# Layer-2 graph sums as three bf16 products, and a message stage with its work moved from VectorE to ScalarE and POOL

## The reference

```python
xn = _layernorm(x, axis=-1)
norm_src = lax.rsqrt(clip(out_deg, 1.0)); norm_dst = lax.rsqrt(clip(in_deg, 1.0))
h_src = xn * norm_src[:, None]
agg = segment_sum(h_src[src], dst)           # sum of messages over a node's in-edges
out = elu((agg * norm_dst[:, None]) @ weight + bias)
```

## Time and profile before

| | |
|---|---|
| Runs of the kernel | 3095.96 us median of 3 (3094.58 to 3096.4) |
| Profiled execution | 3084.4 us, of which the span from first to last instruction is 3082.8 |
| TensorE matmuls (PE) | 2428.9 us busy, 79% of the span |
| Weight loads (PEld) | 1938.2 us, 63% |
| VectorE (DVE) | 1182.7 us, 38% |
| ScalarE (ACT) | 1085.2 us, 35% |
| POOL | 597.3 us, 19% |
| Granted TensorE clock, mean | 0.879 of full speed |

### The profile page before, as it was taken

The page is one execution under the profiler, slowest core; times in us unless marked ns, Lnnn a source line. Parts: engine busy times, 40 slices in busy tenths (PEclk is TensorE's granted clock), DMA queues, the critical chain, the costliest instruction groups (busy, mean ns, idle before and its releaser), DMA issues.

```text
span 3082.8 us, 39405 instructions
## 1 busy us (share of the span) xinstructions
PE 2428.9 (79%) x11905; PEld 1938.2 (63%) x11906; DVE 1182.7 (38%) x2571; ACT 1085.2 (35%) x2028; POOL 597.3 (19%) x482
## 2 busy tenths in 40 slices
PE   0776799989889798876699557968888897925887
PEld 0444688877768677664588435646666666614776
DVE  4444677754635446332001242323342524230111
ACT  3222577755646556532232221121212111112222
POOL 1610011100100101012122111111313223023554
PEclk9887799999898898977799778978989897957999
DMA  3321011110100201024222233212122212053443
GB/s 121 92 79 55 24 45 43 33 63 31 58 31 18 71 30 60 28 80 111 81 75 65 81 129 106 72 47 70 45 70 58 74 46 78 7 142 67 84 86 63
DMA packets 162717, 202.09 MB, mean 66 GB/s; under 512 B 59801, under 2 KB 131120, under 8 KB 162581
## 3 DMA queue, kind: packets, MB, share of 16 engines
q0 software_dynamic: 75168, 89.11, 12.5%
q1 hardware_dynamic: 75834, 100.45, 9.8%
q10 hardware_dynamic: 11578, 10.82, 1.1%
HBM read 108.51 MB, written 93.74 MB: 66 GB/s over the span
## 4 chain that ended last, share of the span: by engine, by line
PE 42%; DMA 38%; another core or an unknown queue 7%; DVE 4%; ACT 3%; issue 2%; SPq 1%; POOL 1%; ACTq 0%; DVEq 0%; POOLq 0%
PE bank L713 39%; DMA agg_rows<-agg_t 34%; PE bank L719 3%; DMA arena<-agg_rows 1%; POOL w_adj L565 1%; SPq L403 1%; DMA xg<-expert_rows 1%; DMA arena<-in_x 1%; DMA feat<-xg 1%; ACT count_a L1167 0%; ACT w_qc L1167 0%; ACT agg_t L1184 0%; DVE arena L1879 0%; ACT w_adj L1166 0%
## 5 line engine op out<-in xcount | busy, mean ns | idle before, releaser
L713 PE MATMUL bank<-xg,w_adj 125*125 125x256 f32 (+1 forms) x2500 | 656.9, 401 | 0.0
L713 PEld LDWEIGHTS bank<-xg,w_adj 125*125 125x125 f32 x2500 | 458.3, 196 | 64.7 <-issue 1.2
L713 PEld LDWEIGHTS bank<-arena,row_hot 128*125 128x125 f32 x3200 | 423.2, 198 | 88.2 <-issue 68.0
L713 PE MATMUL bank<-arena,row_hot 128*125 128x100 f32 x3200 | 431.0, 281 | 47.1 <-remote 19.6
L719 PE MATMUL bank<-ident,arena 125*128 125x125 f32 (+1 forms) x650 | 139.1, 337 | 338.0 <-remote 178.6
L713 PE MATMUL bank<-t,w_h 128*128 128x250 f32 (+1 forms) x1184 | 325.8, 428 | 17.6 <-remote 11.4
L719 PEld LDWEIGHTS bank<-ident,arena 125*128 125x128 f32 (+1 forms) x650 | 85.1, 167 | 389.3 <-issue 383.2
L1560 DVE TENSOR_TENSOR row_hot<-iota_all,arena 128x2000 f32<-128x2000 f32 x100 | 223.7, 2237 | 224.7 <-PE bank L713 221.8
L1166 ACT ACTIVATE w_adj<-bank 125x200 f32<-125x200 f32 x400 | 217.5, 544 | 259.3 <-PE bank L713 254.0
L713 PEld LDWEIGHTS bank<-t,w_h 128*128 128x128 f32 x1184 | 229.6, 199 | 109.9 <-issue 57.9
L713 PE MATMUL bank<-w_adj,arena 128*125 128x256 f32 x1024 | 241.5, 394 | 0.0
(11 more groups left out here) (322 smaller groups left out, 2939.1 us busy)
## 6 DMA issues: line engine op xcount, KB each, us to landing
count_a<-counts POOLq DMA_DIRECT2D x25, 781.2 KB, 6.3
sorted_in<-pad_rows POOLq DMA_DIRECT2D x16, 878.4 KB, 16.9
arena<-sorted_in SPq DMA_DIRECT2D x49, 251.0 KB
counts<-count_a SPq DMA_DIRECT2D x13, 781.2 KB
counts<-w_qc SPq DMA_DIRECT2D x12, 781.2 KB
arena<-rows_b SPq DMA_DIRECT2D x5, 1875.0 KB
w_adj<-in_L_ffn_Wd POOLq DMA_DIRECT2D x8, 1024.0 KB, 6.2
w_adj<-in_L_ffn_W POOLq DMA_DIRECT2D x16, 512.0 KB, 5.8
```

The source lines that it names most:

```text
L713: return pe.matmul(o, w, r, start=first, stop=last, skip_group_check=not check)
```

## The change

Part 1, the sums of layer 1. `adj1` is a bf16 tile, into which the counts are loaded without a cast; the tiles `count_cur[0]` and the semaphores around it are no longer used there. The messages are split into three bf16 parts whose sum is the fp32 number: `part0` = bf16(m), `part1` = bf16(m - part0), `part2` = the rest. `part0` (with the column of ones) and `part1` lie in the space of `xg`, `part2` in the upper half of `w_adj`. Each product becomes three bf16 matmuls into the same bank. The first two count loads are issued together, ahead of the message stage; the load for block b + 1 is issued behind the gather of block b as before, but with no load one block further ahead. Instead of clearing a semaphore, `aggregate` waits for the number of loads landed (`nth`).

Part 2, the message stage. ScalarE takes the root with epsilon as its bias straight from the variances, normalises `h` into `n_big`, makes the fp32 messages in one of two staging tiles (`stage`, in the space of `row_hot`), and copies them as bf16 to `part0`. POOL makes the two other parts (`message_parts`). VectorE keeps the residual sum, the statistics and two small ops. SP stores `feat1` from the staging tile. TensorE's projection steps wait for `msg_full` where they waited for `nodes_full`.

```diff
+        adj1 = [w_adj[0:B, NB * 64 * i:NB * 64 * (i + 1)].bitcast(BF16).rearrange("p (c d) -> p c d", c=NB) for i in range(2)]
+        part2 = w_adj[0:B, NB * 128:NB * 256].bitcast(BF16).rearrange("p (c d) -> p c d", c=NB)
+        parts = xg[:, 0:NB, :].bitcast(BF16)
+        part0, part1 = parts[:, :, 0:D + 1], parts[:, :, D + 2:2 * D + 2]
...
             for s in range(NS):
                 sp.wait_ge(msg_full, s + 1)
-                sp.dma_start(rows(feat1, s), xg[:, G * s:G * s + G, 0:D]).then_inc(msg_stored, 16)
+                sp.dma_start(rows(feat1, s), stage[s % 2]).then_inc(msg_stored[s % 2], 16)
...
             def adjacency_in(b):
 
-                pool.wait_ge(count_in, 16 * (b + 1))
                 if b >= 2:
                     take(pool, adj_used[b % 2])
-                pool.tensor_copy(adj[b % 2], count_cur[0]).then_inc(counts_copied, 1)
-                take(pool, counts_copied)
-                pool.sem_inc(adj_in[b % 2], 1)
-                if b + 1 < NB:
-                    counts_in(b + 1)
+                pool.dma_start(flat(adj1[b % 2]), counts[b * B:b * B + B, :]).then_inc(adj_in[b % 2], 16)
+
+            def message_parts(s):
+
+                at = slice(G * s, G * s + G)
+                pool.wait_ge(msg_full, s + 1)
+                pool.memset(part0[:, at, D:D + 1], 1.0)
+                chain(pool.tensor_tensor(rest, stage[s % 2], part0[:, at, 0:D], ALU.subtract))
+                chain(pool.tensor_copy(part1[:, at, :], rest))
+                chain(pool.tensor_tensor(part2[:, at, :], rest, part1[:, at, :], ALU.subtract))
+                pool.sem_inc(parts_made, 1)
+                chain.restart()
...
             pool.wait_ge(counts_kept, 1)
-            counts_in(0)
-            adjacency_in(0)
-            pool.wait_ge(msg_stored, 16 * NS)
+            for b in range(2):
+                adjacency_in(b)
+            for s in range(NS):
+                message_parts(s)
+            for k in range(2):
+                pool.wait_ge(msg_stored[k], 16 * ((NS + 1 - k) // 2))
...
-                            mm(ps_agg[0:B, 0:cols], adj[par][:, c, 0:B], xg[:, c, 0:cols], False, False, False)
+                            if layer == 0:
+                                mm(ps_agg[0:B, 0:D], adj[par][:, c, 0:B], xg[:, c, 0:D], False, False, False)
+                            else:
+                                mm(ps_agg[0:B, 0:D + 1], adj1[par][:, c, 0:B], part0[:, c, :], False, False, False)
+                                mm(ps_agg[0:B, 0:D], adj1[par][:, c, 0:B], part1[:, c, :], False, False, False)
+                                mm(ps_agg[0:B, 0:D], adj1[par][:, c, 0:B], part2[:, c, :], False, False, False)
...
             def project1(s):
 
-                pe.wait_ge(nodes_full, s + 1)
+                pe.wait_ge(msg_full, s + 1)
...
                 if s == 0:
-                    pe.wait_ge(msg_full, NS)
-                aggregate(s, s % 2, 1, total)
+                    pe.wait_ge(parts_made, NS)
+                aggregate(s, s % 2, 1, total, nth=s // 2)
...
             def messages(s):
 
+                take(act, act_in)
+                act.activation(sd[:, :], mv[:, :, 1], ACT.Sqrt, bias=eps[:, :]).then_inc(act_out, 1)
                 act.wait_ge(nodes_full, s + 1)
                 for i in range(G):
                     b = G * s + i
-                    last = act.activation(xg[:, b, 0:D], n_big[:, b, :], ACT.Copy, scale=inv_out[:, b:b + 1])
+                    last = act.activation(n_big[:, b, :], h_big[:, b, :], ACT.Identity, bias=shift[:, i:i + 1],
+                                          scale=rs[:, i:i + 1])
                 chain(last)
+                if s >= 2:
+                    act.wait_ge(msg_stored[s % 2], 16 * (s // 2))
+                    act.wait_ge(parts_made, s - 1)
+                for i in range(G):
+                    b = G * s + i
+                    last = act.activation(stage[s % 2][:, i, :], n_big[:, b, :], ACT.Copy, scale=inv_out[:, b:b + 1])
+                chain(last)
+                chain(act.activation(part0[:, G * s:G * s + G, 0:D], stage[s % 2], ACT.Copy))
                 act.sem_inc(msg_full, 1)
...
                 chain(last)
-                norm(n, h)
+                norm_sums(h)
+                dve.sem_inc(act_in, 1)
+                take(dve, act_out)
+                chain(dve.reciprocal(rs[:, :], sd[:, :]))
+                chain(stt(out=shift[:, :], in0=mv[:, :, 0], scalar=-1.0, in1=rs[:, :], op0=ALU.mult, op1=ALU.mult))
                 dve.sem_inc(nodes_full, 1)
```

More of the change, by code:

```diff
@@ L186, in program @@
         adj = [w_adj[0:B, NB * 128 * i:NB * 128 * (i + 1)].rearrange("p (c d) -> p c d", c=NB) for i in range(2)]
+        adj1 = [w_adj[0:B, NB * 64 * i:NB * 64 * (i + 1)].bitcast(BF16).rearrange("p (c d) -> p c d", c=NB) for i in range(2)]
+        part2 = w_adj[0:B, NB * 128:NB * 256].bitcast(BF16).rearrange("p (c d) -> p c d", c=NB)
+        parts = xg[:, 0:NB, :].bitcast(BF16)
+        part0, part1 = parts[:, :, 0:D + 1], parts[:, :, D + 2:2 * D + 2]
+        stage_all = row_hot[0:B, :, :, :].rearrange("p k j n -> p (k j n)")
+        stage = [stage_all[:, G * D * k:G * D * k + G * D].rearrange("p (i d) -> p i d", i=G) for k in range(2)]
+        rest = stage_all[:, 2 * G * D:3 * G * D].rearrange("p (i d) -> p i d", i=G)
         near_i = w_adj[0:B, 0:NB * B].bitcast(I32).rearrange("p (b e) -> p b e", e=B)
@@ L258, in program @@
         st2 = sb("st2", [128, 2])
+        eps, shift = sb("eps", [B, 1]), sb("shift", [B, G])
         table_of = sb("table_of", [1, 1])
@@ L549, in _ @@
             chain(pool.tensor_copy(ident_b[:, :], ident[:, :]))
+            chain(pool.memset(eps[:, :], LN_EPS))
             chain(pool.memset(xg[:, :, D:D + 1], 1.0))
@@ L615, in gather @@
                         bass.IndirectOffsetOnAxis(ap=idx_tail[:, 0:1], axis=0)).then_inc(tail_full, 16)
-                if layer == 1 and b + 1 < NB:
+                if layer == 1 and 2 <= b + 1 < NB:
                     adjacency_in(b + 1)
@@ L795, in first_adjacency, with aggregate @@
                         adjacency(k, q)
-            def aggregate(b, par, layer, before, groups=ALL, first=False, last=False):
+            def aggregate(b, par, layer, before, groups=ALL, first=False, last=False, nth=None):
                 cols = D + layer
@@ L1045, in _ @@
             pe.wait_ge(l_c, 16 * 7)
-            aggregate(NQ - 1, (NQ - 1) % 2, 1, total)
+            aggregate(NQ - 1, (NQ - 1) % 2, 1, total, nth=(NQ - 1) // 2)
             def beside(stage, b, plan):
+                step, b = b
                 for j, groups in plan.get(stage, ()):
-                    aggregate(b + j, j % 2, 1, total, groups, last=plan is LAST and j == NL - 1)
+                    aggregate(b + j, j % 2, 1, total, groups, last=plan is LAST and j == NL - 1,
+                              nth=step * (AP // 2) + (NQ + j) // 2)
             def mixer(b, plan):
@@ L1108, in _ @@
             with pe.Fori(0, NS - 1) as p:
-                mixer(p * AP + NQ, MID)
-                graph(p * AP + NQ, MID)
-            mixer(NB - NL, LAST)
-            graph(NB - NL, LAST)
+                mixer((p, p * AP + NQ), MID)
+                graph((p, p * AP + NQ), MID)
+            mixer((NS - 1, NB - NL), LAST)
+            graph((NS - 1, NB - NL), LAST)
             experts(1, lambda e: w1e_sb[e % 2], lambda e: w2e_sb[e % 2], J1)
@@ L1332, in _ @@
             for s in range(NS):
-                root(sd[:, :])
                 messages(s)
```

12 lines of the change are left out of this document (5 added, 7 removed).

## The result

| | before | after |
|---|---|---|
| median of 16 runs each | 3094.94 us | 3071.87 us |
| range | 3078.70 to 3107.24 | 3060.82 to 3089.24 |
| ratio, 95% interval | | 0.993 (0.9909 to 0.995) |
| profiled execution, span | 3084.4, 3082.8 us | 3061.0, 3059.4 us |
| mean granted clock | 0.879 | 0.867 |

The change is faster by 23 us in the medians, inside the range of the forecast and in its direction, but 38 us were forecast. What follows asks where 15 us went.

The account below looks back on a forecast made before the run. TensorE was taken as the bound on average but not everywhere, with SP binding the message stage. Savings of 6.9 + 30.8 + 4.1 less 4 gave 38 us off 3095.96, so 3058 us, range 3022 to 3080.

Parts of the forecast that it names:

- The price of a block: Layer-1 sums: 75 bf16 matmuls at 111 ns take 8.3 us a block, 2.8 us less than 50 fp32 records.
- Pass 0: First of the four middle passes: 1.6 + 1.6 + 1.6 + 2.0, together 6.8 us saved.
- heads stage: Slot of each middle pass with the HI part of a block's products: 1.6 us saved.
- removed cast: Each middle pass: VectorE's 3.46 us op no longer held by POOL's cast; 2.0 us saved, bounds 0.3 and 3.1.
- "norm", "aggs" and "elu": Middle-pass slots where TensorE already waits for VectorE or its one-hot: zero saved.
- Passes 1 to 3: Remaining middle passes: 8.0 us saved in each, each middle pass about 136 us.
- Steps 2 to 4: Projection steps running on TensorE: the tail starts 2.3 us earlier in each, 6.9 us saved together.
- The message stage: Stage bound by SP's transfers: new buffer waits and POOL contention with VectorE cost +4 us, bounds -1 and +15.
- The last pass: Final pass: 2.8 us in "heads", zero in "norm", 1.3 in "sums"; together 4.1 us saved.
- all of it passes: Rival: every block's saving reaches the total, 82 us less, 3014 us; chance 0.08.
- serialised message stage: Rival: ScalarE's shift waits for POOL's whole sequence, 13 us a step; 3069 us, 3075 with lower clock; chance 0.16.
- unhidden weight load: Rival: bf16 weight loads run in series with matmuls, 216 ns a pair, 16.2 us a block; 3181 us; chance 0.08.

Follow-up runs that it names:

- E1: Changed kernel, but POOL begins a step's ten scatters only after VectorE's two row adds of the following pass; ratio to the kernel before 0.9904.
- E2: Changed kernel with VectorE's two row adds of the next pass made in the elu stage of the pass before; ratio to the kernel before 0.9885, median 3057.66 us.
- E5: Changed kernel with 25 one-element memsets ahead of VectorE's loop, putting it where it stood in the kernel before; ratio to the kernel before 0.9893.
- E6: Changed kernel with VectorE normalising the messages again, bf16 sums kept; ratio to the kernel before 0.9862, median 3045.05 us.
- E8: Changed kernel without POOL's two subtractions: second message part a bf16 copy, third set to zero; ratio to the kernel before 0.9908.
- E10: Changed kernel with three one-element memsets ahead of VectorE's loop, which then lies 22 instructions earlier than in the kernel before; ratio to the kernel before 0.9863.
- E7: Kernel before with only ScalarE's normalising in the message stage, sums still fp32, VectorE's loop 25 instructions earlier; ratio to the kernel before 1.0016.
- E4: Changed kernel with the third product of every block made twice, 25 records more a block; ratio to the kernel before 1.0011.
- E3: Changed kernel without the third product of every block, 25 records fewer a block; ratio to the kernel before 0.9915.

## Why the prediction was right or wrong

- **The price of a block: right.** 112 ns each for 75 records, against 111 taken and 8.3 us forecast. The weight load hides. By one line of the Trainium skill, TensorE: Matmul & The Clock Gate, Part 3 "The mechanism", a load overlaps matmuls in flight only when the row group differs; the trace disagrees, with loads recorded at 143 ns under records that follow each other every 112. The same section also lets a load that targets the background weight buffer be pulled ahead, and with that the trace is in line; my prediction built its rival on the narrower line alone.
- **Pass 0: right**, 7.7 for 6.8 us: 1.5 in the heads stage (1.6 forecast), 2.2 in the middle (1.6), 3.1 in the "elu" stage (from 10.2 to 7.1 us, likewise in every pass; 2.0 forecast for the removed cast) and 0.9 in "ranks" (1.6). "norm", "aggs" and "elu" gave nothing but longer waits. That the sum came out within 1 us is partly luck: pass 0 takes 136.2 to 139.2 us in E1, E2, E5, E6, E8 and E10, none of which stalls there.
- **Passes 1 to 3: the step that failed.** I summed "8.0 each" with "VectorE's chain to the next rows" taken from the trace before, as if a loop's jump had a fixed price. VectorE's first add waits 9 us there, with the place of its loop, and the passes got 3.3, 3.5 and 2.8 us. Without the stall (E5) passes 1 and 2 are 6.5 and 6.9 us shorter than before, and at "about 136 us" as forecast. What is then left of the 8.0 is in the middle stage, where E5 gains nothing (79.4 for 79.1 us in pass 1, with 64 products of the hidden layer at 21.48 us for 20.47). The trace before couldn't show the stall; the diff could have warned: it took instructions out ahead of a loop.
- **Steps 2 to 4: mis-sized.** "2.3 us each" came out at 1.0, 1.0 and, at the end of TensorE's work in step 4, 2.6. The sums take 2.7 us less, but TensorE waits 0.32 us for the one-hot, and w_qc takes 14.20 and 14.29 us for 13.14 and 13.15 in steps 2 and 3 (in step 4, 14.34 for 14.83): its windows in step 2, changed kernel and before,

```profile
1896.91:1911.04 14.13, 14.13 (x42) 7.77 (x41) 5.13 (x9) 0.44 (x2) 0.00 (x0) 0.92 0.17 42
```

```profile
1892.78:1905.85 13.07, 13.07 (x43) 7.41 (x41) 5.12 (x9) 0.56 (x2) 1.37 (x2) 1.00 0.26 63
```

  have a granted clock of 0.92 and 1.00. I allowed for the clock in "aggs" and "elu", and not here. Of the 4.6 us that TensorE is ahead after step 4, 1.6 are lost before pass 0, where VectorE waits 34.3 us for the rows (32.5 before).
- **The message stage: wrong in sign.** +4 forecast with bounds of -1 and +15, -3.6 measured (with steps 0 and 1). The waits stood as told (SP issues back to back from 1774.0 on, ScalarE waits 2.5, 1.4 and 1.9 us for a free buffer in steps 2 to 4, VectorE's first projection step still waits for the rows' storing), but the contention is hidden (E8). I had also read the earlier trace rows as showing that POOL's cast and VectorE's op did not overlap; their records there lie over each other, and only the later trace shows the op lasting to the end of POOL's. The gain comes with the bf16 sums, in SP's queue: the issue of the first rows takes 24.5 us for 26.2 and that of wn 31.8 for 34.2. All bf16 kernels here have the short ones, E7 the long ones; why stays open.
- **The last pass: right in number, and that looks like luck.** Of the 7.2 us of the last stretch, pass 3 has 2.8 (its heads, middle, "elu" and, as in pass 2, 0.9 of the rest), so 4.4 are left for 4.1 forecast. But by the same count E7, whose sums are still fp32, gains 4.7 us there, E5 0.5 and E10 nothing, so the gain can't be put down to shorter sums. The waits for the one-hot in "norm" and "sums" are now 2.87 and 1.35 us:

```profile
2620.75 0.69 PE L726 MATMUL bank<-xg,oh_tail 125*125 125x257 f32 x2 [2.87 <-DVE oh_tail L1640]
...
2675.47 0.69 PE L726 MATMUL bank<-xg,oh_tail 125*125 125x257 f32 x2 [1.35 <-DVE oh_tail L1640]
```

- **The rivals.** Not all of it passes: E4 puts the slope at 25 us of 68, E3 at none of 68. The serialised message stage and the unhidden weight load did not come.

In the rows the forecast of 38 us met 30.9 (all but the unchanged start), the medians 23; the start differs by up to 17.5 us between traces and the runs of one kernel by 28 us, so the gap of 8 is no finding. That 30.9 is as near to 38 as it is has luck in it too: passes 1 to 3 lack 14.4 us and steps 2 to 4 another 3.9, while the message stage brought 7.6 and the rest 2.6 more than forecast.

## What to carry to other kernels

A change that adds or removes instructions ahead of a loop moves the loop, and here VectorE waited 9 us at each of three jumps back, or not at all, by that alone; some 3.3 us of each wait reached the length of the pass. When a wait with no releaser appears at a loop's head as often as the loop jumps back, shift the loop by a few harmless instructions before explaining it by anything else. And price a shorter TensorE stage only up to the point where another engine becomes the last one: beyond it the idle lowered the clock here, and steps 2 and 3 of E3 were slower with fewer products.

## What the runs showed of the hardware

- A jump back of VectorE's loop brought no stall with the loop in one place (also 22 instructions earlier) and one of 8.6 to 10.0 us 25 instructions earlier, with packets of the instruction queue around it; in the fp32 kernel it was 5.4 to 6.5 us, with packets too.
- TensorE idle for 2.99 us was followed by 6 us at a granted clock of 0.50 (E3, steps 2 to 4; 20 records took 4.67 us instead of 2.50).
- POOL takes 2.53 us for a two-input fp32 subtraction of 1280 elements and 1.25 us for a cast of as many, from the groups by line of the changed kernel.
